# Weights laid out by partition, and w2, the scale and shift weights and w_in issued on ScalarE's DMA queue

## The reference

```python
h = _noise_encoding(t, E)                 # E = 128
h = jax.nn.silu(h @ W1 + b1)              # (16, 512)
h = h @ W2 + b2                           # (16, 512)
scale = (h @ Wsc + bsc)[:, None, :]       # (16, 1, 256)
shift = (h @ Wsh + bsh)[:, None, :]
out = jax.nn.silu(scale * _layer_norm(x, gamma, beta) + shift)
out = out @ W_in + b_in
out = jax.nn.silu(scale * _layer_norm(out, gamma, beta) + shift)
out = out @ W_out + b_out
return out + x
```

## Time and profile before

| what | value |
|---|---|
| median of 3 runs | 93.65 us (93.6 to 96.47) |
| the profiled execution, its own time | 93.97 us |
| its span (first to last recorded instruction) | 91.9 us |
| PE busy | 82.4 us, 90% of the span |
| DVE busy | 65.8 us, 72% |
| ACT busy | 56.2 us, 61% |
| POOL busy | 42.9 us, 47% |
| HBM read | 7.65 MB |

### The profile page before, as it was taken

How to read it: one execution, slowest core, us unless ns; L and a number is a source line. 1 busy time by engine, 2 the same in 40 slices (tenths; PEclk the granted TensorE clock), 3 DMA queues, 4 the chain that set the end, 5 groups by cost and what they waited for, 6 DMA issues and landing times. The chain is left out here.

```text
span 91.9 us, 1285 instructions
## 1 busy us (share of the span) xinstructions
PE 82.4 (90%) x348; PEld 43.8 (48%) x350; DVE 65.8 (72%) x176; ACT 56.2 (61%) x169; POOL 42.9 (47%) x50
## 2 busy tenths in 40 slices
PE   4999869879899399899999999699999999999970
PEld 1366527326654165356446552454554455544450
DVE  1637497897799999992996895369566663959370
ACT  5103100497948998993898682969949964845400
POOL 3000301891389976893899679639608003030000
PEclk9999999999999999999999999999999999999999
DMA  1989999999100000003200500060023006023353
GB/s 27 272 274 385 392 356 393 391 404 388 61 0 0 0 0 4 0 0 114 99 22 0 214 14 4 0 228 0 0 97 131 0 0 228 4 111 117 115 207 135
DMA packets 6311, 11.92 MB, mean 130 GB/s; under 512 B 673, under 2 KB 2465, under 8 KB 6305
## 3 DMA queue, kind: packets, MB, share of 16 engines
q1 hardware_dynamic: 6304, 11.85, 35.6%
HBM read 7.65 MB, written 4.19 MB: 129 GB/s over the span
## 5 line engine op out<-in xcount | busy, mean ns | idle before, releaser
L277 ACT ACTIVATE act<-act,cond 128x256 f32<-128x256 f32 x64 | 35.6, 589 | 5.4 <-POOL act L219 2.3
L592 PE MATMUL acc<-act,win_sb 128*128 128x512 f32 x64 | 31.7, 615 | 2.1 <-ACT act L277 2.1
L592 PE MATMUL acc<-act,wout_sb 128*128 128x512 f32 (+1 forms) x68 | 29.1, 572 | 0.0
L297 ACT ACTIVATE squares<-acc,shift 128x256 bf16<-128x256 f32 x32 | 15.1, 471 | 10.4 <-issue 6.6
L592 PEld LDWEIGHTS acc<-act,wout_sb 128*128 128x128 f32 x68 | 12.6, 190 | 13.1 <-issue 12.4
L592 PEld LDWEIGHTS acc<-act,win_sb 128*128 128x128 f32 x64 | 10.8, 191 | 10.7 <-issue 8.0
L198 POOL TENSOR_TENSOR rstd<-var,minus_half 128x2 f32<-128x2 f32 (+1 forms) x7 | 5.7, 821 | 20.4 <-DVE var L374 20.4
L410 DVE SCALAR_TENSOR_TENSOR act<-acc,shift,gamma_sb 128x256 f32<-128x256 f32 x32 | 13.9, 476 | 1.7 <-ACT squares L297 1.5
L202 POOL TENSOR_TENSOR rstd<-var,minus_half 128x2 f32<-128x2 f32 x8 | 6.5, 816 | 16.6 <-DVE var L403 16.6
L426 DVE SCALAR_TENSOR_TENSOR o_sb<-acc,const_sb,x_sb 128x512 f32<-128x512 f32 (+1 forms) x17 | 11.8, 715 | 3.2 <-PE acc L592 3.1
L214 POOL TENSOR_TENSOR act<-act,gamma_sb 128x512 f32<-128x512 f32 x9 | 11.9, 1326 | 0.9
(11 more groups left out here) (56 smaller groups left out, 57.5 us busy)
## 6 DMA issues: line engine op xcount, KB each, us to landing
x_sb<-x_dram SPq DMA_DIRECT2D x8, 512.0 KB, 10.1
out_dram<-o_sb SPq DMA_DIRECT2D x15, 256.0 KB, 2.0
w_sb<-w_dram SPq DMA_DIRECT2D x1, 1024.0 KB, 7.9
wss_sb<-wsc_dram SPq DMA_DIRECT2D x1, 512.0 KB, 9.6
wss_sb<-wsh_dram SPq DMA_DIRECT2D x1, 512.0 KB, 10.5
w_sb<-w_dram SPq DMA_DIRECT2D x1, 256.0 KB, 3.7
gamma_sb<-gamma_dram SPq DMA_DIRECT2D x1, 256.0 KB, 8.1
beta_sb<-beta_dram SPq DMA_DIRECT2D x1, 256.0 KB, 10.6
```

The source lines that it names most:

```text
L277: return nc.scalar.activation(buf[:, c, b], buf[:, c, b], ACT.Silu, bias=cond[:, 1, c, i:i + 1], scale=cond[:, 0, c, i:i + 1], **kw)
L297: nc.scalar.activation(squares[:], y_slot(p, c)[:, b], ACT.Square, bias=shift2[:, p, c, b:b + 1], accum_out=sumsq[:, p, c, b:b + 1]).then_ ...
L592: mm = nc.tensor.matmul(bank_of(name)[:, b:b + n].rearrange("p b s -> p (b s)"), w[:, k, c * P:(c + 1) * P], act_in[:, k, b:b + n].rearran ...
```

## The change

The host prepares w2, w_in and w_out in the order in which the partitions hold them, and stacks the scale and shift weights into one array of the same kind. So each partition's share is one piece of memory: 8 KB for w2, 8 KB for the stacked weights (one DMA in place of two, one semaphore `wss_in` in place of two), 2 KB each for w_in and w_out. The DMAs of w2, of the stacked weights and of w_in leave SP's list and stand at the head of ACT's, before the load of the function table. w_out stays on SP. The bytes are the same.

```diff
         def _(sp):
...
             load_x(0)
-            sp.dma_start(w2_sb[:], w2.rearrange("(k p) n -> p k n", p=P)).then_inc(w2_in, 16)
             sp.dma_start(gamma_sb[:], gamma).then_inc(gamma_in, 16)
             load_x(1)
-            sp.dma_start(wss_sb[:, :, 0, :], wsc.rearrange("(k p) n -> p k n", p=P)).then_inc(wsc_in, 16)
-            sp.dma_start(wss_sb[:, :, 1, :], wsh.rearrange("(k p) n -> p k n", p=P)).then_inc(wsh_in, 16)
             sp.dma_start(beta_sb[:], beta).then_inc(beta_in, 16)
-            sp.dma_start(win_sb[:], w_in.rearrange("(k p) n -> p k n", p=P)).then_inc(win_in, 16)
             load_x(2)
             load_x(3)
-            sp.dma_start(wout_sb[:], w_out.rearrange("(k p) n -> p k n", p=P)).then_inc(wout_in, 16)
+            sp.dma_start(wout_sb[:], w_out).then_inc(wout_in, 16)
...
         def _(act):
+            act.dma_start(w2_sb[:], w2).then_inc(w2_in, 16)
+            act.dma_start(wss_sb[:], wss).then_inc(wss_in, 16)
+            act.dma_start(win_sb[:], w_in).then_inc(win_in, 16)
             nc.scalar.preload_act_table_set("silu_and_others")
...
             pe.wait_ge(h2_ready, 1)
-            pe.wait_ge(wsc_in, 16)
-            pe.wait_ge(wsh_in, 16)
+            pe.wait_ge(wss_in, 16)
...
+    def rows_by_partition(a):
+        a = np.asarray(a)
+        return np.ascontiguousarray(a.reshape(-1, P, a.shape[1]).transpose(1, 0, 2))
...
-        "w2": np.ascontiguousarray(L0_cond_W2),
-        "wsc": np.ascontiguousarray(L0_cond_Wsc),
-        "wsh": np.ascontiguousarray(L0_cond_Wsh),
+        "w2": rows_by_partition(L0_cond_W2),
+        "wss": np.ascontiguousarray(np.stack([rows_by_partition(L0_cond_Wsc), rows_by_partition(L0_cond_Wsh)], axis=2)),
...
-        "w_in": np.ascontiguousarray(L0_cond_W_in),
-        "w_out": np.ascontiguousarray(L0_cond_W_out),
+        "w_in": rows_by_partition(L0_cond_W_in),
+        "w_out": rows_by_partition(L0_cond_W_out),
```

More of the change, by code:

```diff
@@ L54, with build @@
 N_CONST = COL_PICK + KH * B
-def build(nc, x, consts, w1, w2, wsc, wsh, gamma, beta, w_in, w_out, out):
+def build(nc, x, consts, w1, w2, wss, gamma, beta, w_in, w_out, out):
     with ExitStack() as ctx:
@@ L119, in build @@
         const_in, w1_in, w2_in = sem("const_in"), sem("w1_in"), sem("w2_in")
-        wsc_in, wsh_in, win_in, wout_in = sem("wsc_in"), sem("wsh_in"), sem("win_in"), sem("wout_in")
+        wss_in, win_in, wout_in = sem("wss_in"), sem("win_in"), sem("wout_in")
         gamma_in, beta_in = sem("gamma_in"), sem("beta_in")
```

## The result

The changed kernel takes 101.47 us (median of 4 runs, 100.21 to 103.55) beside 94.14 us for the kernel before (median of 4). The ratio is 1.070, with a 95% interval of 1.061 to 1.080: slower by 7%. The ratio leaves out each kernel's executions that lay more than 1.5% above its fastest (96.47 us before; 101.93 and 103.55 us after, with a mean granted clock of TensorE of 0.93 and 0.92 beside 0.97 in the fastest). The profiled execution took 100.21 us with a span of 98.4 us.

What follows compares the result with a forecast made beforehand. The prediction took the landing of x pair 0 and 11.5 us of fixed-order work to bound the opening. All terms were 0 except 3.9 us for w2 beside x pair 0: 93.65 + 3.9 = 97.5 us, range 94.0 to 101.0.

Steps and rivals of the forecast that it cites:

- the 11.5 us: Opening, landing of x pair 0 to first SiLU: said to stay 11.5 us; a change would mean the forecast was wrong.
- What bounds the kernel: Opening: x pair 0 lands at 6.13 us, then 11.5 us of fixed-order work leads to the first SiLU at 17.65.
- rival 4: Opening: faster, below 91.8 us, would need x pair 0 landing 1.9 us sooner, at 4.2; chance 3%.
- Weights by partition: Weight loads: 1536 fewer pieces, larger ones moving slightly slower, 0.34 us over unwaited loads; taken as 0 on the path.
- Issue time on ACT: ACT's opening: three issues of 1.3 to 2.1 us delay the table load, which still ends before the sine; cost 0.
- w2 beside x pair 0: Opening loads: ACT's queue shares the engines by equal packets, so x pair 0 lands at 10.0 us; cost 3.9 us.
- w1 ... still ahead of 6.26: PE's first layer: w1 under equal packets lands at 6.1 us, before the warm products end at 6.26; no cost.
- The clock: Rival on PE's opening: equal packets plus a clock fall after 3.7 us empty, 99.5 to 102 us; chance 20%.
- From the opening to the end: Main loop: no wait is for a load, so the first SiLU's shift of 3.9 us passes on whole.
- Equal bytes: Rival on the opening loads: queues share by bytes, cost 0.8 to 2.7 us, 94.4 to 96.4 us; chance 28%.
- no cost: Rival on the opening loads: ACT's issues come later or SP's line is served first, 93.5 to 94.1 us; chance 11%.
- faster: Rival on the opening: an earlier x pair 0 pulls the first SiLU ahead of 17.65, below 91.8 us; chance 3%.

Runs made afterwards that it cites:

- queue_only: The kernel before, old layout, with the DMAs of w2, the scale weights, the shift weights and w_in moved to the head of ACT's list: ratio 1.042.
- after_sine: The changed kernel with ACT's three DMA issues (w2, stacked weights, w_in) moved behind the sine: ratio 1.072.
- win_alone: The changed kernel with only w_in at the head of ACT's queue, w2 and the stacked weights back on SP: median 98.07 us.
- w2_alone: The changed kernel with only w2 on ACT's queue, the stacked weights and w_in back on SP: ratio 1.035.
- table_first: The changed kernel with ACT's three DMA issues placed after the load of the function table: ratio 1.074.

## Why the prediction was right, and where its numbers were off

The direction and the main mechanism were right: slower, through w2 and the stacked weights beside x pair 0. I forecast 97.5 us, 4.1% above 93.65; it is 7.0% by the ratio, or 100.2 us, near the upper end of the range (101.0), and the median of all four executions, 101.47, lies just above it. By one of its own signs the forecast was wrong: the 11.5 us did change, to 12.95, because the clock took over. And the first SiLU is at 23.98, not 21.5. By the prediction's own steps:

- **What bounds the kernel**, the landing of x pair 0 and then 11.5 us of work in fixed order: right for a later landing. For an earlier one it was not: PE's own list was as late as this path, and with x pair 0 landing 1.5 us sooner only 0.35 were won. So the 1.9 us sooner of rival 4 would hardly have made the kernel faster.
- **Weights by partition**, taken as 0: right, 0.996 (0.993 to 1.000). The packets fell from 6304 to 4752, by the 1552 forecast. The step read the price of small pieces from the wrong rows, though: the scale and shift weights, in pieces of 1 KB, landed at 13.5 and 14.9 us, and from 10 to 14 us the rate was 374 and 357 GB/s, below the 393 that was used. It cost nothing, since no engine waited for them.
- **Issue time on ACT**, 0 on the path: right in its sum, 1.4 us for three issues, the table loaded by 3.4. But the sine was then late all the same, at 6.81, for a reason that this step did not look at: its constants.
- **w2 beside x pair 0**, the packets' turns: the way of sharing is shown (42 to 44, 40 to 39, and 95 to 96 with small pieces). The term was mis-sized: x pair 0 at 11.0 and not 10.0, 4.90 us and not 3.9. The sum let the turns begin with w1. In fact the constants ran beside w2 already, and w1 beside the stacked weights, so ACT's queue had moved 2.32 MB and not 2.10 by then: 0.22 MB more, by my estimate half of the missing microsecond. The other half is the pace, 0.38 MB a us from 1.83 to 10.2 and not 0.40, for up to 3 us hardly 0.2 MB had gone. Of the step's own bounds, 3.9 to 5.8, I had taken the lowest. The 400 GB/s that it expected until 8 us were 286 (213 before).
- **"w1 ... still ahead of 6.26"**: this step failed. By the same slip I gave it 1.05 MB of company; it had all of w2 and nearly all of the stacked weights (1.95 MB by 8 us), and landed at 8.9. On its own it cost nothing, x pair 0 being later still, but it emptied PE for 2.52 us.
- **The clock**: left to a rival (20%), with an empty stretch of 3.7 us ahead of `mean1(0)` as its cause. It fell, but not there: at about 10.1 us, after the 2.52 us for w1 (a wait that the step on w1 had ruled out) and before the wait ahead of `mean1(0)`, which was 1.08 us. It cost 1.43 us of the opening and nothing of the loop, less than the 2 and up to 4 of the rival. So the truth was the forecast with its rival's clock, at less than the rival's price. That PE's waits together are the cause is shown by the run that filled them: the clock stayed up, and it was 11.2 us in place of 12.95.
- **From the opening to the end**, passed on whole: right to the hundredth, 6.33 at the first SiLU and 6.33 at the last chain.
- *Equal bytes*, *no cost* and *faster* are refuted by the packet counts and the ratio.

What the Trainium skill has in "DMA: Bandwidth & Descriptors" ("Queues, rings and completion order") of the turns at packet boundaries agrees with the runs here wherever both queues move (42 packets beside 44, 95 beside 96). The page gives several descriptors to a packet; in these counts each turn is one contiguous piece of one partition. Of how a DMA on one queue waits for earlier issues on the other, the turns alone say nothing: they would give x pair 0 at 6.8 in queue_only (8.9 measured) and w2 at 8.5 to 9.5 in after_sine (12.9). Why it waits stays open. The runs show only that it does, longer the more stands in front, and in queue_only the turns had given 0.7 of the 2.8 us that x pair 0 lost.

## What to carry to other kernels

In this kernel a second DMA queue added no bandwidth once the engines were full (399 to 406 GB/s from 8 to 16 us, 357 to 414 in the kernel before); it reordered. Per turn each queue moved one packet, so a queue of 8 KB pieces had four fifths of the bytes beside one of 2 KB pieces, and the load that heads the critical path must not stand beside it. Keep one queue in the order of need; putting just the first-needed load on the second gained nothing here (1.000). And count what a wait does to TensorE's clock as well as what it does to the path.

## What was not expected of the hardware

- A DMA's first packet waited here for much of what was issued before it on the other queue: w1, issued at 1.16, began at 4.7 to 5.1 behind 1 MB, at 3.9 to 4.2 behind 0.52 MB, at 2.9 behind 0.26 MB, and at 2.2 with one queue; w2, issued at 4.26 on an empty queue, began just before 8.0.
- TensorE's granted clock went to half after PE had been empty for as little as 0.81 us (win_alone, the fall 1.2 us after the wait), though not always: the kernel before has a wait of the same length ending at 13.90 us, with the clock at 1.00.
- The pace of PE's first products hangs on little. The same twelve took 5.30 us in the kernel before and in the changed one, 4.25 in w2_alone and 4.28 in table_first, one execution each. With twelve products of zeros and x pair 0 on ACT's queue it had doubled by 7.97 us (three products in 0.81), with ten it was still the lower one at 9.7 (1.44).
- ACT's DMA issue did not wait for its table load (table_first): the issue began at 0.74 us, the load ran from 0.71 to 1.99.
